# Summing 32 weighted rows per node by three strided reductions, and ordering the vector engine by drains

## The reference

```
feat = einsum('ni,rhid->rnhd', layernorm(x), conv_weights)   # 3750 nodes, 8 relations, 4 heads x 64
e    = leaky_relu(el[type, src] + er[type, dst])             # one score per edge and head, 123750 edges
alpha = exp(e - segment_max(e, dst)) / segment_sum(...)      # softmax over the edges into a node
h    = segment_sum(alpha * feat[type, src], dst) + h_bias
x    = x + h
out  = x + sum over the top-2 experts of  cw[n, e] * (gelu(ln(x) @ W1[e] + b1[e]) @ W2[e] + b2[e])
```

## Time and profile before

| | |
|---|---|
| median of 3 runs | 1859.76 us (1859.42 to 1861.65) |
| the profiled execution | 1861.03 us, span 1859.3 us |
| PE, busy share of the span | 70% |
| PEld | 56% |
| DVE | 70% |
| ACT | 42% |
| POOL | 78% (982 gathers of rows in the 30 windows) |
| mean granted TensorE clock | 0.84 |

### The profile page before, as it was taken

One profiled execution on the slowest core, in us unless ns is written; L12 is line 12 of the kernel. 1 busy time (PEld: TensorE's weight loads), 2 busy tenths in 40 slices (PEclk: granted clock), 3 DMA queues, 4 the chain that ended last, 5 costly groups with the idle time before them and its releaser, 6 DMA issues.

```text
span 1859.3 us, 29421 instructions
## 1 busy us (share of the span) xinstructions
PE 1296.2 (70%) x6881; PEld 1047.7 (56%) x6881; DVE 1300.4 (70%) x2578; ACT 782.7 (42%) x2829; POOL 1459.5 (78%) x2201
## 2 busy tenths in 40 slices
PE   6999940017686678777758676867777685858587
PEld 3444410017575567666757565757666575757576
DVE  7660032459888888887868686869687877878681
ACT  3544410205454444544544453535444444545442
POOL 0726758868888888888888888888888888888830
PEclk9999975558788788988878888888889787888789
DMA  8758576323433333333333333333333333333310
GB/s 229 223 159 219 165 209 197 95 74 96 94 96 97 92 98 96 97 96 97 96 97 95 96 97 97 95 96 97 97 95 94 96 97 97 96 96 96 94 36 7
DMA packets 86798, 204.28 MB, mean 110 GB/s; under 512 B 32427, under 2 KB 44645, under 8 KB 82323
## 3 DMA queue, kind: packets, MB, share of 16 engines
q0 software_dynamic: 57504, 147.97, 29.5%
q10 hardware_dynamic: 9596, 33.95, 6.0%
q1 hardware_dynamic: 19485, 20.52, 4.0%
HBM read 162.22 MB, written 40.16 MB: 109 GB/s over the span
## 4 chain that ended last, share of the span: by engine, by line
POOL 44%; DVE 14%; issue 14%; PE 7%; POOLq 3%; ACT 2%; DVEq 1%; DMA 0%; ACTq 0%; SPq 0%
POOL rows L901 31%; POOL space_ring L933 10%; DVE fold_ps L1079 3%; PE y_ps L1513 3%; PE hid_ps L1499 3%; DVE rows L1075 2%; POOL space_edge L933 2%; ACT rows L1402 2%; POOL out_dram L909 1%; DVE xo L1236 1%; DVE er_hot L1032 1%; DVE score L1034 1%; POOL xrows L901 1%; DVE rden L1064 1%; POOLq L914 1%
## 5 line engine op out<-in xcount | busy, mean ns | idle before, releaser
L901 POOL DMA_INDIRECT rows<-table,idx_st x982 | 946.0, 963 | 183.0 <-issue 180.6
L1513 PE MATMUL y_ps<-w,hT 128*128 128x256 f32 x1920 | 522.5, 430 | 287.8 <-ACT hT L1392 287.8
L1513 PEld LDWEIGHTS y_ps<-w,hT 128*128 128x128 f32 x1920 | 400.0, 215 | 373.3 <-ACT hT L1392 312.3
L1499 PE MATMUL hid_ps<-zT,w 128*128 128x128 f32 x3840 | 490.6, 290 | 0.0
L1499 PEld LDWEIGHTS hid_ps<-zT,w 128*128 128x128 f32 x3840 | 480.2, 206 | 13.5 <-issue 10.0
L1402 ACT ACTIVATE rows<-rows,ex 128x65 f32<-128x65 f32 x1320 | 326.1, 346 | 111.2 <-DVE ex L1066 111.2
L1392 ACT ACTIVATE hT<-hid_ps,b1t 128x128 f32<-128x128 f32 x960 | 272.8, 366 | 207.2 <-PE hid_ps L1499 207.2
L1079 DVE TENSOR_TENSOR fold_ps<-rows,fold_ps 128x780 f32<-128x780 f32 (+1 forms) x348 | 326.3, 938 | 28.3 <-DVE rows L1075 5.0
L933 POOL MEMSET space_ring<- 128x280 uint8 x838 | 292.2, 349 | 0.4
L587 PE MATMUL feat_ps<-wc,xnT 128*125 128x512 f32 x480 | 220.6, 604 | 1.4 <-ACT xnT L522 1.4
L1075 DVE TENSOR_TENSOR rows<-rows,fold_ps 128x2340 f32<-128x2340 f32 (+1 forms) x76 | 189.7, 2529 | 3.8 <-DVE rows L1075 3.8
(11 more groups left out here) (199 smaller groups left out, 1145.5 us busy)
## 6 DMA issues: line engine op xcount, KB each, us to landing
table<-stage ACTq DMA_DIRECT2D x30, 924.0 KB
rows<-table,idx_st POOLq DMA_INDIRECT x982, 2.8
w<-in_L_ffn_W_dram SPq DMA_DIRECT2D x16, 512.0 KB
node_row<-ranked SPq DMA_DIRECT2D x30, 132.0 KB
table<-stage ACTq DMA_DIRECT2D x30, 107.2 KB
x_all<-in_x_dram SPq DMA_DIRECT2D x2, 1120.0 KB
wc<-_L_gnn_conv_weights_dram ACTq DMA_DIRECT2D x2, 1024.0 KB, 7.9
attnb<-in_L_gnn_attn_l_dram SPq DMA_DIRECT2D x1, 1024.0 KB, 12.3
```

The costliest lines, as they stand in the source:

```text
L901: q.indirect_dma_start(buf[:, k, :], None, table, bass.IndirectOffsetOnAxis(idx[:, col + k:col + k + 1], 0)).then_inc(landed, 16)
L1499: last = t.matmul(hid_ps[e % 2][:, m * P:m * P + n], w1[:, e, k, m * P:(m + 1) * P], zT[:, k, 0:n], start=(k == 0), stop=(k == KD - 1))
L1513: last = t.matmul(y_ps[p % 2][0:n, (e % 2) * D:(e % 2 + 1) * D], hT[e % 2][:, k, 0:n], w2[:, e, k, :], start=(k == 0), stop=(k == KH - 1))
```

## The change

1. `lanes` in PSUM and the additions onto it go. DVE weighs slots 0 to 20 in place in `rows` (two instructions, 12 and 9 slots), and three TENSOR_REDUCE (`summed`) sum slots 0 to 11, 12 to 20 and 21 to 31. Each reads `rows` with the slot innermost: for each of the 260 columns it reads 12, 9 or 11 floats that lie 264 floats (1056 bytes) apart. The first two sums go to PSUM (`part`), the third to `acc`, onto which both parts are then added.
2. In windows with a degree over 32, slots 32 to 39 are added in one TENSOR_TENSOR onto slots 12 to 19 of `rows`; both of its inputs lie in SBUF.
3. `Steps` becomes `Drains` on DVE in all functions of the windows but `mix`: a wait is a drain instruction of the engine, and the instructions raise no semaphore of their own. Signals to other engines stay (`begun`, `ex_ok` are new names for two of them).
4. ACT raises `gelu_ok` once per expert, behind the last of its four Gelus, and PE waits for the expert's number.
5. `freed` is raised behind slots 0-11, behind slots 12-20, and by two behind slots 21-31.

```diff
+class Drains:
+    def __init__(self, eng):
+        self.eng, self.n = eng, 0
+    def did(self, ins):
+        self.n += 1
+    def wait(self):
+        self.eng.drain()
...
-    lanes = fold_ps[:, 0:LANES * AGG].rearrange("p (k c) -> p k c", k=LANES)
+    part = [bank("part_ps")[:, 0:AGG], fold_ps[:, at:at + AGG]]
...
         def front(w, par, half):
-            st = Steps(dve, front_step, w * N_FRONT)
+            st = Drains(dve)
...
-        def add(par, lo, n=LANES):
-            return v.tensor_tensor(lanes[:, 0:n], rows[par][:, lo:lo + n, 0:AGG], lanes[:, 0:n], ALU.add)
+        def summed(par, lo, hi, out):
+            return v.tensor_reduce(out, rows[par][:, lo:hi, 0:AGG].rearrange("p k c -> p c k"), AX_X, ALU.add)
         def weigh_all(w, par, st, between):
-            st.did(weighted(par, 0, LANES, lanes))
-            st.did(weighted(par, LANES, 12))
+            st.did(weighted(par, 0, 12))
             st.did(weighted(par, 12, ACT_LO))
...
                 weighted(par, PAIRED * SLOTS, NS)
                 dve.drain()
-                for lo, n in ((32, 3), (35, 3), (38, 2)):
-                    add(par, lo, n)
-                    dve.drain()
-            for lo in (3, 6):
-                st.did(add(par, lo))
-                st.wait()
+                v.tensor_tensor(rows[par][:, 12:12 + SLOTS, 0:AGG], rows[par][:, 12:12 + SLOTS, 0:AGG],
+                                rows[par][:, PAIRED * SLOTS:NS, 0:AGG], ALU.add)
+                dve.drain()
+            st.did(summed(par, 0, 12, part[0]))
+            st.wait()
             dve.sem_inc(freed, 1)
-            for lo in (9, 12, 15):
-                st.did(add(par, lo))
-                st.wait()
+            st.did(summed(par, 12, ACT_LO, part[1]))
+            st.wait()
             dve.sem_inc(freed, 1)
-            st.did(add(par, 18))
             between()
+            st.wait()
             dve.wait_ge(act_weighed, w + 1)
-            st.wait()
-            st.did(add(par, 21))
-            st.wait()
-            dve.sem_inc(freed, 1)
-            for lo in (24, 27):
...
-            st.did(add(par, 30, 2))
...
-            st.did(v.tensor_copy(acc_f, lanes[:, 0]))
-            st.wait()
-            st.did(v.tensor_tensor(acc_f, acc_f, lanes[:, 1], ALU.add))
-            st.wait()
-            v.tensor_tensor(acc_f, acc_f, lanes[:, 2], ALU.add).then_inc(acc_ok, 1)
+            st.did(summed(par, ACT_LO, ACT_HI, acc_f))
+            st.wait()
+            dve.sem_inc(freed, 2)
+            st.did(v.tensor_tensor(acc_f, acc_f, part[0], ALU.add))
+            st.wait()
+            v.tensor_tensor(acc_f, acc_f, part[1], ALU.add).then_inc(acc_ok, 1)
...
             for m in range(KH):
-                a.activation(hT[e % 2][:, m, 0:n], ..., bias=b1t[:, e, m:m + 1]).then_inc(gelu_ok, 1)
+                last = a.activation(hT[e % 2][:, m, 0:n], ..., bias=b1t[:, e, m:m + 1])
+            last.then_inc(gelu_ok, 1)
```

More of the change, by code:

```diff
@@ L722, in phase2 @@
     gate_ps, zt_ps = bank("gate_ps"), bank("zt_ps")
-    fold_ps = env["ctx"].enter_context(nc.psum_tensor("fold_ps", [P, 1024], F32))
-    lanes = fold_ps[:, 0:LANES * AGG].rearrange("p (k c) -> p k c", k=LANES)
-    at = LANES * AGG
+    fold_ps = bank("fold_ps")
+    at = 0
     ex_ps = fold_ps[:, at:at + H * NS].rearrange("p (h k) -> p h k", h=H)
@@ L728, in phase2 @@
     er9 = [fold_ps[:, at + i * H * R1:at + (i + 1) * H * R1].rearrange("p (h r) -> p h r", h=H) for i in range(2)]
-    assert at + 2 * H * R1 <= 1024
+    at += 2 * H * R1
+    part = [bank("part_ps")[:, 0:AGG], fold_ps[:, at:at + AGG]]
+    assert at + AGG <= 512
     b2_ps = zt_ps[:, 256:256 + D]
@@ L760, in phase2 @@
     xblk_ok, xblk_in = sem("xblk_ok"), sem("xblk_in")
[L761 to L765, removed]
+    mix_step, begun, ex_ok = sem("mix_step"), sem("begun"), sem("ex_ok")
     def after(eng, s, value):
@@ L1057, in front @@
             alone(dve, dve_passed)
-            assert st.n == N_FRONT
         def exps(w):
-            st = Steps(dve, ex_step, w * N_EX)
+            st = Drains(dve)
             dve.wait_ge(den_ok, w + 1)
@@ L1065, in exps @@
             st.wait()
-            st.did(v.tensor_scalar(ex[:], rden[:], 2.0, -1.0, ALU.mult, ALU.add))
+            v.tensor_scalar(ex[:], rden[:], 2.0, -1.0, ALU.mult, ALU.add).then_inc(ex_ok, 1)
             st.did(v.tensor_scalar(ex_ps, rden[:], 2.0, -1.0, ALU.mult, ALU.add))
@@ L1129, in further @@
         def further(j, par, col):
-            st = Steps(dve, xfront_step, j * N_XFRONT + 1)
+            st = Drains(dve)
             st.wait()
@@ L1140, in further @@
             st.did(v.tensor_copy(xebuf[:, :, SLOTS], m_new[:]))
-            assert st.n == N_XFRONT
-            st = Steps(dve, xex_step, j * N_XEX + 1)
+            st = Drains(dve)
             dve.wait_ge(xden_ok, j + 1)
@@ L1161, in post @@
         def post(w, par, half):
-            st = Steps(dve, post_step, w * N_POST)
+            st = Drains(dve)
             st.did(v.reciprocal(r4[:], acc[:, :, HD]))
@@ L1181, in post @@
             rsqrt_column_steps(nc, st, rstd2[:], varp[:], hcol[:], tmp1[:])
-            assert st.n == N_POST, st.n
             v.tensor_scalar(z[:], xo[par][:], mv2[:, 0:1], rstd2[:, 0:1], ALU.subtract, ALU.mult).then_inc(z_ok, 1)
         def gate_in_steps(u):
-            st = Steps(dve, gate_step, u * N_GATE)
+            st = Drains(dve)
             dve.wait_ge(logit_ok, u + 1)
@@ L1247, in further_chunk @@
             dve.reg_add(chunks, chunks, 1)
-            st = Steps(dve, chunk_step, n * N_CHUNK)
+            st = Drains(dve)
             def go(ins):
@@ L1307, in prepare @@
             front(w, par, half)
-        for s in (xfront_step, xex_step):
-            dve.sem_inc(s, 1)
         dve.sem_inc(xfolded, 1)
@@ L1391, in gelu @@
             for m in range(KH):
-                a.activation(hT[e % 2][:, m, 0:n], hid_ps[e % 2][:, m * P:m * P + n], ACT.Gelu,
-                             bias=b1t[:, e, m:m + 1]).then_inc(gelu_ok, 1)
+                last = a.activation(hT[e % 2][:, m, 0:n], hid_ps[e % 2][:, m * P:m * P + n], ACT.Gelu,
+                                    bias=b1t[:, e, m:m + 1])
+            last.then_inc(gelu_ok, 1)
         def weigh(w, par, lo, hi):
             if lo == ACT_LO:
-                act.wait_ge(ex_step, w * N_EX + 2)
+                act.wait_ge(ex_ok, w + 1)
             for k in range(lo, hi):
@@ L1488, in node_scores @@
             pe.wait_ge(xnwT_ok, w + 1)
-            after(pe, begin_step, w * N_BEGIN)
+            after(pe, begun, w)
             for k in range(KD):
@@ L1494, in hidden @@
         def hidden(u, e, n=P):
-            after(pe, gelu_ok, (u * NE + e - 1) * KH)
+            after(pe, gelu_ok, u * NE + e - 1)
             for m in range(KH):
```

29 lines of the change are left out of this document (9 added, 20 removed).

## The result

| | kernel before | changed kernel |
|---|---|---|
| median, 4 runs each | 1860.7 us (1859.42 to 1863.51) | 1999.4 us (1996.55 to 2002.43) |
| ratio of the times | | 1.0743 (95%: 1.072 to 1.0767) |
| profiled execution | 1861.03 us, span 1859.3 | 1997.29 us, span 1995.6 |
| `e_diff` of window 1 to window 29 | 1361.1 us | 1488.6 us |
| from there to the end | 75.5 us | 81.4 us |

A forecast was written before the change was run, and what follows sets the result against it. POOL's issuing of gathers was taken to bound the kernel before, with DVE near, and DVE's chain the changed one: 1861.0 + 208 + 2 - 66.3 - 21.7 + 3.6 + 5 = 1991.6, so 1990 us; range 1880 to 2040.

The forecast's parts named there:

- 208 + 2 - 66.3 - 21.7: 28-window stretch: DVE work +208 us, further slots +2, waits for gathered rows -66.3 and for PE -21.7 go.
- sums, weighing, branch: DVE, per window: sums +6.2 us, weighing about -0.1, and in windows with the branch -0.5.
- drains and other gaps, further slots: DVE: drains outside the sums +1.5 us a window; further slots of windows 0, 2 and 4 add 2 us.
- waits for rows: DVE's 66.3 us of waiting for gathered rows over 28 windows go as its chain grows.
- The price of the stride: New reductions cost 1.89 ns an element, as L462; bounds 1.04 and 2.08; sums take 17.7 us instead of 11.55.
- The drains: 34 DVE waits a window outside the sums, each 0.04 to 0.05 us dearer as drains: +1.5 us a window.
- PE's 21.7 us "vanish": DVE's waits for PE at mix pair 1 and pair 3, 21.7 us in all, go because DVE arrives later.
- Unchanged instructions: DVE instructions that the change leaves alone: no change of length was counted, 0 us.
- Head and tail: Head, up to `e_diff` of window 1: +3.6 us; tail, after `e_diff` of window 29: +5 us.
- The signs: Changed profile: reductions 6.0, 4.6, 5.6 us; two windows about 104 us; one gather beside each L1097 lasting 2 to 3 us.
- Both that were tied to the dense price: Reductions at dense price: gather queue held 16 times, 1887 us, chance 0.12; queue not held, not slower, 1860 us, chance 0.06.
- the forecast's example: Kernel before: gather beside L1149, 2080 elements from SBUF, took 2.68 us, not 0.95, ending 0.83 us after it.

The follow-up runs named there:

- E2: Changed kernel, reductions reading contiguous neighbours and the branch addition taking its second input from PSUM: 1860.55 us, ratio 1.0005.
- E12: Kernel before, with the memset between two gathers halved (140 bytes per partition instead of 280): 1773.9 us, ratio 0.9548.
- E9: Kernel before, with the three reductions and the 8-row branch addition alone, VectorE's signals kept in place of drains: 1945.4 us, ratio 1.0456.
- E3: Changed kernel, with the batch count's register load moved ahead of the drain of the second reduction: 1967.4 us, ratio 1.058.
- E1: Changed kernel, with the three reductions reading contiguous neighbours (other elements summed), branch addition still with two SBUF inputs: 1886.6 us, ratio 1.0144.
- E10: Kernel before, with the branch's three lane additions replaced by one addition of 2080 elements, both inputs in SBUF: 1878.45 us, ratio 1.0098.

## Why the prediction was right

**The bound and its turn.** POOL before, VectorE after, as the waits and the chain show. E2 and E12 hold it from both sides.

From `e_diff` of window 1 to that of window 29, 122 us were forecast (208 + 2 - 66.3 - 21.7) and the stretch grew by 127.5. VectorE's busy time and gaps, taken apart in both traces, tell where:

| part of the stretch | forecast | measured |
|---|---|---|
| sums, weighing, branch | +166 | +141.7 |
| drains and other gaps, further slots | +44 | +34.1 |
| waits for rows | -66.3 | -66.3 |
| gaps ahead of the mixes | -21.7 | +6.6 |
| length of the unchanged instructions | 0 | +11.4 |

**The price of the stride.** I took 1.89 ns an element from the only strided reduction in the trace; it was 1.82. The three reductions together are 15.6 us instead of 16.2, and all of the sums 16.75 instead of 17.7. With the weighing and the branch that is -24 us over 28 windows.

**The drains.** Forecast 1.5 us a window; all gaps outside the sums and the mixes grew by 1.2, with small waits for PE that went, and E9 gives 1.4. The term was 0.1 to 0.3 us a window too large.

**PE's 21.7 us "vanish".** This step failed in its sum. The waits for PE went, but the register load came into the open at the same mix, 1.0 us in each of 28 windows: +28. The prediction followed what VectorE does to instructions with data, and not what ran behind `add(18)` on its queue. E3 gives the size, 20 us of gaps.

**Unchanged instructions.** I counted their length as unchanged. Together they took 11 us more. As far as `z` shows, that is because the new order sets some of them beside a gather that holds them.

These misses, -24, -10, +28 and +11, sum to +5, which is what the forecast of the stretch was short by. That the time came within 10 us of the forecast (1999.4 against 1990) is in good part this cancelling, and so luck: the two larger misses alone are over 20 us each.

**Head and tail.** `e_diff` of window 1 comes 2.9 us later (forecast 3.6), and the tail is 5.9 us longer (forecast 5). PE waited 3.7 us for `z` there, where 3.1 were forecast.

**The signs.** The reductions at L1084 took 5.8, 4.4 and 5.4 us (named: 6.0, 4.6 and 5.6), two windows are 106.3 us (named: 104), and 15 of the 16 additions L1097 had a gather of 2.0 to 2.8 us beside them (named: one each, 2 to 3); in one window no gather ran there.

**The rivals.** Both that were tied to the dense price came out at their numbers once the price was made dense: 1887 with the held queue (E1: 1886.6), 1860 without (E2: 1860.6). The held gather can be seen in the changed kernel too, beside an addition that ran from 1140.95 to 1143.28:

```profile
1140.50 0.95 POOL L909 DMA_INDIRECT rows<-table,idx_st  x1 [0.16 <-issue]
...
1141.97 2.13 POOL L909 DMA_INDIRECT rows<-table,idx_st  x1 [0.17 <-issue]
```

It ends at 1144.09, 0.82 us after the addition, as the 0.83 us of the forecast's example. It costs nothing there, since VectorE is the bound.

## What to carry to other kernels

Fewer instructions are no gain if each one reads in steps of 16 bytes or more: price the access pattern from the nearest row of the trace, and count how much cover the engine has before its work turns into time. When an edit puts a wait, drain or signal, in another place, look at everything that ran under the instruction ahead of it, register loads too, and move those ahead of the wait. And an edit's cost holds for one bound only: the same drains cost 1.4 us a window or nothing, depending on who was waited for.

## What the runs showed of the hardware that I had not expected

- VectorE, fp32 from SBUF: eight to a sum, 2.33 us for 2080 elements at strides of 1 and 2 floats, 3.67 to 3.87 from 4 to 260; two to a sum at 260 floats apart, the dense price.
- VectorE stood 1.0 us at a register load from SBUF behind a wait for the instruction ahead, be it a drain (the changed kernel) or a signal (E9), and 0.3 us there with the load moved ahead of the drain (E3).
- An addition of 2.33 us with both inputs in SBUF holds the gather that starts beside it until 0.8 to 0.9 us after its own end; over 16 additions that was 1.1 (changed kernel), 1.3 (E10) and 1.6 us (E1) each, and with the second input in PSUM (E2) nothing that can be measured.
- It goes the other way too: `z`, a TENSOR_SCALAR of 256 elements that takes 412 ns, ended 0.11 us after the gather's end, up to 961 ns long, in all 24 of 30 cases of the changed kernel in which it started more than 0.1 us into a gather.
- The same kernel took 1860 us in some sessions and 2095 to 2102 in others, and halving the spacing of the gathers changed it by a factor of 0.95 in the first and 1.19 in the second.
